# Newton-Schulz in a fast-weight kernel: its first gram from the raw momentum, and four filler stages at other places

## The chip, the cores and the metric

One core of a Trainium2 chip. The metric is the device time in microseconds (us) of one execution, the median of three runs of the kernel before.

## The reference

`x` is 2048 x 256. After a layer norm (`xn`), three things are added: `x + attn(xn) + ffn(xn)`. The attention part has a windowed softmax attention and a test-time-training layer (TTT) with four heads. TTT goes through the sequence in 16 chunks of 128 rows. In each chunk it uses its fast weights W0, W1, W2 (64 x 64 for each head), then updates them. The update is what the change touches:

```python
def _newtonschulz5(G):
    X = G
    X = X / (jnp.sqrt(jnp.sum(X * X, axis=(1, 2), keepdims=True)) + 1e-07)
    for a, b, c in NS_COEFFS:            # five of them
        A = X @ X.transpose(0, 2, 1)
        B = b * A + c * (A @ A)
        X = a * X + B @ X
    return X

def step(carry, xi):
    ...
    dw0 = dw0 + M0 * mm                  # gradient plus momentum, the same for dw1, dw2
    M0n, M1n, M2n = (dw0, dw1, dw2)
    dw0 = _newtonschulz5(dw0)
    ...
    return ((renorm(W0 + dw0, n0), ..., M0n, M1n, M2n), out)
```

The feed-forward part is a mixture of 32 experts (weights `w1`, `w2`, relu squared, routing by the top 8) and a shared expert of inner size 512, also relu squared.

## The kernel before, in words

All is float32. The sequence is taken in 16 blocks of 128 rows. Each engine has its program written out by hand, in order, and semaphores tie them together; an instruction whose semaphore is not there holds all that stands behind it on its engine. `body(i, last)` of each engine does block i and prepares block m = i + 1. The last block has no update, so there are 15 updates.

The 12 matrices of an update (4 heads x 3) are held as two groups g = 0, 1. A group is 128 partitions (two heads, one in the low 64, one in the high 64) by 3 matrices by 64 columns: `Mom[g]` (gradient plus momentum), `X[g]`, `Am[g]` (the gram), `Mp[g]`. Products of single heads are matmuls of 64x64 tiles, in one or the other quarter of the array. The PSUM of a group is `CC[g]`, two banks, `CA[g]` and `CB[g]`.

The way into Newton-Schulz, on each engine:
- TensorE: `grads` (L682) writes the six gradients of a group into CA. Then come `h_up(i, 2)`, `shared_up(i, 0)`, `sums(i, 0)`, `sums(i, 1)`, `shared_up(i, 1)` and `h_up(i, 3)`. `sums` (L693) adds the squares of a head's rows over its partitions, with a matmul by a matrix of ones in blocks.
- VectorE: `grad` (L1100) makes Mom, its squares (L1109) and their row sums (L1112). `sum_copy` (L1114) copies the summed squares from PSUM. `x_first` (L1118) adds 1e-7 to the root, takes the reciprocal and multiplies Mom by it, which is X.
- POOL (GpSimd): `ss_pow` (L335) takes the square root, as a power of 0.5.

Then come 20 stages, `st` = 0 to 19, four for each of the five steps, each done for g = 0 and g = 1. In stage 0 TensorE turns X (`ns_turn`, L697, two transposes) and ACT copies the turned one to SBUF (`xt`, L476). In stage 1 TensorE takes the gram (`ns_gram`, L703, six matmuls of 64x64) and VectorE copies it to Am (`ns_a`, L1129). In stage 2 TensorE multiplies Am by Am and VectorE makes Mp = b/c Am + the product (`ns_m`, L1134). In stage 3 TensorE multiplies Mp by X, and VectorE makes the next X (`ns_x`, L1142), with a times X from POOL (`ax`, L339).

Between the stages stands other work, the fillers. A dictionary `fill` on each engine says what follows which stage, and they have to be in the same order where they share a buffer:
- `h_up(i, u)` (L825) is the up projection of four experts into the PSUM bank HB, of which there is only one. ACT reads it with a relu into `hr` (`h_relu`, L507), and POOL squares it into `hq` (`h_sq`, L358). `y_down(i, u)` (L833) multiplies hq by the down weights into YB, and VectorE adds that to `acc` (`y_acc`, L1321).
- `shared_up` (L815) is the shared expert's up projection into M0, in two parts; ACT's `shared_relu` (L503) and POOL's `shared_sq` (L354) follow.
- `ln_norm(m)` (L998) makes `xn` of the next block on VectorE from the statistics and `rstd`, which POOL's `prep_rstd` (L287) gives. `att_scale` (L1217) scales the turned q and k with four VectorE instructions (aqT, akT). In stage 0 VectorE does these two. TensorE's `q_out` (L751), in the fillers of stage 2, waits for `e_aT` of att_scale; `prep_turn(m)` (L632) behind it begins the work on the next block.

POOL's own order in this part is k_u twice, `h_sq(i, 1)`, `ss_pow` twice, `prep_rstd(m)`, `h_sq(i, 2)`, then `ax` twice, `shared_sq`, `h_sq(i, 3)`. The change leaves it alone.

Of the kernel before, what the change touches and what calls it, by code (L numbers as in the profile page):

```python
# [27 lines left out]
ALU = mybir.AluOpType  # L28
# [4 lines left out]
P = 128  # L33
D = 256
KT = D // P
HD = 64
NH = 4
G = 2
# [18 lines left out]
NI = len(NS)  # L57
# [16 lines left out]
def build(nc, x, wall_d, rows_d, wo, fast_d, affine_d, fc1T, fc2T, e1T, e2T, upT, downT, ident_d, fixed_d, out):  # L74
# [3 lines left out]
    with ExitStack() as ctx:  # L78
# [18 lines left out]
        ident = sb("ident", [P, P])  # L97
# [178 lines left out]
        def _(pool):  # L276
# [56 lines left out]
                pool.tensor_tensor(kt[g][:, 3, :], ks[g][:, 1, :], ks[g][:, 2, :], ALU.mult).then_inc(e_ku[g], 1)  # L333

            def ss_pow(i, g):  # L335
                pool.wait_ge(e_sst[g], 3 * i + 1)
                power(r3[g][:, 2, :], r3[g][:, 1, :], half, 3).then_inc(e_pw[g], 1)

            def ax(i, g, it):  # L339
# [75 lines left out]
        def _(act):  # L415
# [12 lines left out]
            def prep_xnT(m):  # L428
                act.wait_ge(e_pt, m + 1)
                a(xnT[:, :, :].rearrange("p k t -> p (k t)"), M0[:, 0:D], ACT.Copy).then_inc(e_xnT, 1)  # L430
# [62 lines left out]
            def q_out(i):  # L493
                act.wait_ge(e_qo, i + 1)
                a(to[:, :], M1[:, 0:D], ACT.Copy)
                a(tsq[:, :], M1[:, 0:D], ACT.Square).then_inc(e_to, 1)
# [6 lines left out]
            def shared_relu(i):  # L503
                act.wait_ge(e_upm, i + 1)
                a(ur[:, :, :].rearrange("p s t -> p (s t)"), M0[:, :], ACT.Relu).then_inc(e_ur, 1)

            def h_relu(i, u):  # L507
                act.wait_ge(e_h, NU * i + u + 1)
                if u > 1 or not (isinstance(i, int) and i == 0):
                    act.wait_ge(e_hq, NU * i + u - 1)  # L510
                a(hr[u % 2][:, :, :].rearrange("p s t -> p (s t)"), HB[:, :], ACT.Relu).then_inc(e_hr, 1)
# [29 lines left out]
            def body(i, last):  # L541
                if last:
                    gate_sig(i)
                    y_first(i)
                    h_relu(i, 2)
                    shared_relu(i)
                    h_relu(i, 3)
                    q_out(i)
                    act.preload_act_table_set("natural_log_exp_and_others")
                    h_relu(i, 4)  # L550
                    probs(i)
                    h_relu(i, 5)
                    probs_T(i)
                    h_relu(i, 6)
                    h_relu(i, 7)
                    comb_T(i)
                    y_T(i)
                    return
                m = i + 1
                k_side(i, 0)  # L560
                k_side(i, 1)
                gate_sig(i)
                y_first(i)
                h_relu(i, 2)

                def to_exp():
                    act.preload_act_table_set("natural_log_exp_and_others")

                def to_sigmoid():
                    act.preload_act_table_set("sigmoid_and_others")  # L570

                shared_relu(i)
                h_relu(i, 3)
                fill = {1: [lambda: h_relu(i, 4)], 2: [lambda: q_out(i), lambda: prep_xnT(m)],
                        5: [lambda: prep_qk(m)], 6: [lambda: prep_v(m)], 7: [lambda: h_relu(i, 5), lambda: prep_small(m)],
                        8: [lambda: prep_sq8(m)], 9: [lambda: prep_vT(m), lambda: h_relu(i, 6), to_exp],
                        11: [lambda: lr_exp(m)], 12: [lambda: prep_qkT(m)],
                        13: [lambda: probs(i)], 14: [lambda: h_relu(i, 7), lambda: lr_ln(m)], 15: [lambda: probs_T(i), to_sigmoid],
                        18: [lambda: comb_T(i)], 19: [lambda: x_lat(m)]}
                for st in range(4 * NI):  # L580
                    if st % 4 == 0:
                        for g in range(G):
                            xt(i, g, st // 4)
                    for f in fill.get(st, []):
                        f()
                h_relu(m, 0)
                y_T(i)
                h_relu(m, 1)
                for g in range(G):
                    w_T(m, g)  # L590
# [24 lines left out]

        @block.tensor
        def _(pe):
            x_turn = [Expect(pe, e_x[g], f"x_turn{g}") for g in range(G)]
            xt_in = [Expect(pe, e_xt[g], f"xt_in{g}") for g in range(G)]
            am_in = [Expect(pe, e_am[g], f"am_in{g}") for g in range(G)]  # L620
            mp_in = [Expect(pe, e_mp[g], f"mp_in{g}") for g in range(G)]
# [71 lines left out]
            def sums(i, g):  # L693
                pe.wait_ge(e_s3[g], 2 * i + 2)
                mm(CB[g][:, 0:3], bdones[:, :], r3[g][:, 0, :]).then_inc(e_ssb[g], 1)

            def ns_turn(g, last_step):  # L697
                x_turn[g].wait(skip=1 if last_step else 0)
                pe.transpose(CA[g][0:HD, 0:P], X[g][:, 0, :], ident[:, :])  # L699
                pe.transpose(CA[g][:, P:2 * P], X[g][:, 1:3, :].rearrange("p w c -> p (w c)"), ident[:, :])\  # L700
                    .then_inc(e_t[g], 1)

            def ns_gram(g):  # L703

                xt_in[g].wait()
                low, high = slice(0, HD), slice(HD, P)

                def gram(out_, rows, n, c):
                    return mm(out_[c, 0:HD], XT[g][rows, n, c], XT[g][rows, n, c])

                gram(CA[g], low, 0, low)
                gram(CB[g], high, 1, high)
                gram(CA[g], low, 0, high)
                gram(CB[g], high, 1, low)
                gram(CA[g][:, 2 * P:], low, 1, low)
                gram(CA[g][:, 2 * P:], low, 1, high).then_inc(e_prod[g], 1)
# [98 lines left out]
            def shared_up(i, part):  # L815

                if part == 0:
                    pe.wait_ge(e_gh, i + 1)
                for c in range(part * SC // 2, (part + 1) * SC // 2):
                    for k in range(KT):  # L820
                        ins = mm(M0[:, c * P:(c + 1) * P], up_s[:, k, c * P:(c + 1) * P], xnT[:, k, :], k == 0, k == KT - 1)
                if part == 1:
                    ins.then_inc(e_upm, 1)
# [42 lines left out]
            def body(i, last):  # L866
# [30 lines left out]
                m = i + 1  # L897
# [5 lines left out]
                grads(i, 0)  # L903
                grads(i, 1)
                h_up(i, 2)
                shared_up(i, 0)
                sums(i, 0)
                sums(i, 1)
                shared_up(i, 1)
                h_up(i, 3)  # L910
                fill = {2: [lambda: q_out(i), lambda: prep_turn(m)], 3: [lambda: y_down(i, 2)],
                        4: [lambda: prep_qk(m)], 5: [lambda: prep_qk_more(m)], 6: [lambda: prep_v(m)],
                        7: [lambda: h_up(i, 5)], 8: [lambda: y_down(i, 3), lambda: prep_mom(m)],
# [6 lines left out]
                for st in range(4 * NI):  # L920
                    for g in range(G):
                        if st % 4 == 0:
                            ns_turn(g, st // 4 == NI - 1)
                            if st == 0 and g == 0:
                                y_down(i, 1)
                        elif st % 4 == 1:
                            ns_gram(g)
                            if st == 1 and g == 0:
                                h_up(i, 4)
                        elif st % 4 == 2:  # L930
                            ns_pair(g, CA, am_in, Am, Am)
                        else:
                            ns_pair(g, CB, mp_in, Mp, X)
                    for f in fill.get(st, []):
                        f()
# [32 lines left out]
        def _(dve):  # L968
# [149 lines left out]
            def x_first(i):  # L1118

                for g in range(G):  # L1120
                    dve.wait_ge(e_pw[g], i + 1)
                    nc.vector.tensor_scalar(r3[g][:, 2, :], r3[g][:, 2, :], 1e-7, None, ALU.add).then_inc(e_sst[g], 1)
                    dve.wait_ge(e_sst[g], 3 * i + 2)
                    nc.vector.reciprocal(r3[g][:, 1, :], r3[g][:, 2, :]).then_inc(e_sst[g], 1)
                    dve.wait_ge(e_sst[g], 3 * i + 3)
                    nc.vector.tensor_tensor(X[g][:, :, :], Mom[g][:, :, :],
                                            r3[g][:, 1, :].unsqueeze(2).to_broadcast([P, 3, HD]), ALU.mult).then_inc(e_x[g], 1)

            def ns_a(i, g, it):  # L1129
                dve.wait_ge(e_prod[g], 3 * NI * i + 3 * it + 1)  # L1130
                nc.vector.tensor_copy(Am[g][:, :, :], CC[g][:, 0:6 * P].rearrange("p (w c) -> p w c", w=3)[:, :, 0:HD])\  # L1131
                    .then_inc(e_am[g], 1)

            def ns_m(i, g, it):  # L1134

# [207 lines left out]
            def body(i, last):  # L1343
# [33 lines left out]
                        17: [lambda: att_out(i)], 18: [lambda: y_acc(i, 7)]}  # L1377
                for st in range(4 * NI):
                    for g in range(G):
                        if st % 4:  # L1380
                            (ns_a, ns_m, ns_x)[st % 4 - 1](i, g, st // 4)
                        if st > 10 and routing:
                            routing.pop(0)()
                    for f in fill.get(st, []):
                        f()
# [68 lines left out]
```

## Time and profile before

| | |
|---|---|
| median of 3 runs | 831.35 us (829.08 to 831.86) |
| the profiled execution | 830.14 us |
| its span, first to last instruction | 828.1 us |
| granted clock of TensorE, mean | 0.996 |
| TensorE busy (matmul) | 780.7 us, 94% |
| VectorE busy | 714.6 us, 86% |
| ScalarE (ACT) busy | 354.0 us, 43% |
| GpSimd (POOL) busy | 406.8 us, 49% |
| chain that ended last | PE 53%, DVE 33%, issue 6%, ACT 5%, POOL 2% |

PE is TensorE, PEld its weight loads, DVE is VectorE. The spans of matmuls are modelled and overlap, so a matmul row's duration is longer than the step from one to the next; the starts are what to go by. All matmuls have line 629, that of the helper `mm`, and all ACT instructions line 426, so that they are told apart by their tiles. A float32 matmul shows as two instructions.

### The profile page before, as it was taken

Reading aid. Unit: us, or ns where it says so; the run is one execution under the profiler, and the core shown is the slowest. Engines: PE = TensorE matmul, PEld = TensorE weight load, DVE = VectorE, ACT = ScalarE, POOL = GpSimd, SP = SyncE. Lnnn points to the kernel's source line nnn. Section 1 sums busy time; section 2 is a strip of 40 time slices with the busy share of each in tenths; the row PEclk is TensorE's granted clock in tenths of the full one; section 3 lists DMA queues with packets and bytes.
Section 4 is the critical chain, followed back from the end, with each engine's and each line's share of the span. In section 5 each row is a group of like instructions: output and inputs, shape, how many; then the busy total and the mean of one; then the engine's idle time right before and its main releaser. Section 6 shows DMA issues by size and latency. Waiting matters only on the chain.

```text
span 828.1 us, 24889 instructions
## 1 busy us (share of the span) xinstructions
PE 780.7 (94%) x9776; PEld 668.5 (81%) x9776; DVE 714.6 (86%) x2592; ACT 354.0 (43%) x868; POOL 406.8 (49%) x535
## 2 busy tenths in 40 slices
PE   3899999999999999999999999999999999999997
PEld 1888888888888888878888788887888888888886
DVE  4789898898988979889798897988979889898876
ACT  2544344443444434444344444444444444434533
POOL 1654555445454454544555445544465444655442
PEclk9899999999999999999999999999999999999999
DMA  8100000000000000000000000000000000000000
GB/s 321 54 3 14 9 2 21 3 13 9 2 21 2 14 8 2 21 2 15 8 3 20 2 15 9 3 21 2 15 8 2 21 2 15 8 2 15 2 15 7
DMA packets 9811, 15.09 MB, mean 18 GB/s; under 512 B 1120, under 2 KB 8928, under 8 KB 9440
## 3 DMA queue, kind: packets, MB, share of 16 engines
q1 hardware_dynamic: 7904, 7.80, 3.2%
q10 hardware_dynamic: 1792, 5.70, 1.8%
q8 instruction: 78, 1.28, 0.6%
q14 instruction: 37, 0.30, 0.1%
HBM read 11.41 MB, written 2.10 MB: 16 GB/s over the span
## 4 chain that ended last, share of the span: by engine, by line
PE 53%; DVE 33%; issue 6%; ACT 5%; POOL 2%; DMA 1%; SPq 0%; DVEq 0%
PE CC L629 18%; PE M L629 13%; PE HB L629 8%; DVE acc L1328 8%; PE YB L629 8%; DVE Wn L1175 4%; DVE Mp L1138 2%; DVE dhb L1094 2%; DVE X L1146 2%; PE CC L699 2%; DVE Am L1131 2%; POOL r L285 2%; DVE sm L1233 1%; DMA rows<-in_rows 1%; PE CC L700 1%
## 5 line engine op out<-in xcount | busy, mean ns | idle before, releaser
L363 POOL TENSOR_TENSOR hq<-hr 128x512 f32<-128x512 f32 x128 | 137.1, 1071 | 71.9 <-ACT hr L426 71.9
L285 POOL TENSOR_TENSOR r<-r,half 128x3 f32<-128x3 f32 (+1 forms) x78 | 77.9, 1011 | 155.1 <-DVE r L1116 67.9
L629 PE MATMUL HB<-xlT,e_s 128*128 128x128 f32 x1024 | 143.0, 283 | 0.4 <-ACT xlT L426 0.4
L629 PE MATMUL YB<-e_s,hq 128*128 128x128 f32 x1024 | 141.3, 281 | 1.8 <-DVE acc L1328 0.8
L629 PEld LDWEIGHTS HB<-xlT,e_s 128*128 128x128 f32 x1024 | 126.7, 193 | 6.8 <-ACT xlT L426 0.7
L1328 DVE SCALAR_TENSOR_TENSOR acc<-YB,cw,acc 128x128 f32<-128x128 f32 x448 | 125.4, 342 | 7.9 <-PE YB L629 7.9
L341 POOL TENSOR_TENSOR aX<-X,a_tile 128x192 f32<-128x192 f32 x150 | 92.9, 640 | 79.9 <-DVE X L1146 79.9
L426 ACT ACTIVATE hr<-HB 128x512 f32<-128x512 f32 x128 | 76.1, 594 | 128.5 <-PE HB L629 128.5
L629 PEld LDWEIGHTS YB<-e_s,hq 128*128 128x128 f32 x1024 | 124.2, 191 | 7.4 <-issue 4.1
L629 PEld LDWEIGHTS CC<-X,Mp 64*64 64x64 f32 x1800 | 58.3, 135 | 23.6 <-issue 11.3
L629 PEld LDWEIGHTS CC<-Am 64*64 64x64 f32 x1800 | 59.5, 134 | 21.8 <-DVE Am L1131 18.2
L426 ACT ACTIVATE XT<-CC 128x256 f32<-128x256 f32 x150 | 50.8, 381 | 59.7 <-PE CC L700 59.5
L629 PE MATMUL CC<-X,Mp 64*64 64x64 f32 x1800 | 68.6, 222 | 7.6 <-DVE Mp L1138 7.6
L629 PE MATMUL CC<-Am 64*64 64x64 f32 x1800 | 69.8, 223 | 1.9
L1146 DVE SCALAR_TENSOR_TENSOR X<-CC,aX 128x192 f32<-128x192 f32 x150 | 51.3, 352 | 13.4 <-PE CC L629 13.3
L629 PE MATMUL M<-wall,xnT 128*128 128x512 f32 (+1 forms) x128 | 56.9, 551 | 3.6 <-DMA rows<-in_rows 3.6
L629 PEld LDWEIGHTS CC<-XT 64*64 64x64 f32 x1800 | 43.2, 133 | 20.7 <-ACT XT L426 14.7
L1131 DVE COPY Am<-CC 128x192 f32<-128x192 f32 x150 | 48.4, 347 | 9.3 <-PE CC L629 8.3
L1138 DVE SCALAR_TENSOR_TENSOR Mp<-Am,CC 128x192 f32<-128x192 f32 x150 | 49.8, 351 | 7.2 <-PE CC L629 3.6
L629 PE MATMUL CC<-XT 64*64 64x64 f32 x1800 | 55.6, 232 | 0.0
L699 PE MATMUL CC<-ident,X 128*64 128x128 f32 x150 | 39.7, 281 | 0.0
L333 POOL TENSOR_TENSOR kt<-ks 128x128 f32<-128x128 f32 x30 | 13.7, 459 | 51.0 <-ACT ks L426 51.0
(180 smaller groups left out, 1525.3 us busy)
## 6 DMA issues: line engine op xcount, KB each, us to landing
xa<-in_x SPq DMA_DIRECT2D x16, 128.0 KB, 2.1
e_s<-in_e1T ACTq DMA_DIRECT2D x1, 2048.0 KB, 12.7
e_s<-in_e2T ACTq DMA_DIRECT2D x1, 2048.0 KB, 19.3
xr<-in_x SPq DMA_DIRECT2D x16, 128.0 KB, 2.2
out<-ot SPq DMA_DIRECT2D x16, 128.0 KB, 1.7
wall<-in_wall SPq DMA_DIRECT2D x1, 820.0 KB, 7.1
up_s<-in_upT ACTq DMA_DIRECT2D x1, 512.0 KB, 15.9
down_s<-in_downT ACTq DMA_DIRECT2D x1, 512.0 KB, 20.0
```

The costliest lines, as they stand in the source:

```text
L285: return pool.tensor_tensor(dst, src, expo[:, 0:n], ALU.pow)
L341: pool.tensor_tensor(aX[g][:, :, :].rearrange("p w c -> p (w c)"), X[g][:, :, :].rearrange("p w c -> p (w c)"), a_tile[:, it, :], ALU.mult ...
L363: pool.tensor_tensor(hq[b][:, :, :], hr[b][:, :, :], hr[b][:, :, :], ALU.mult).then_inc(e_hq, 1)
L426: return nc.scalar.activation(out_, in_, func, **kw)
L629: return pe.matmul(out_, lhsT, rhs, start=start, stop=stop)
L699: pe.transpose(CA[g][0:HD, 0:P], X[g][:, 0, :], ident[:, :])
L1094: tt(dhb[g][:, :], kt[g][:, 0, :], dhi[g], ALU.mult)
L1131: nc.vector.tensor_copy(Am[g][:, :, :], CC[g][:, 0:6 * P].rearrange("p (w c) -> p w c", w=3)[:, :, 0:HD])\
L1138: nc.vector.scalar_tensor_tensor(Mp[g][:, :, :].rearrange("p w c -> p (w c)"), Am[g][:, :, :].rearrange("p w c -> p (w c)"), b / c, CA[g][ ...
L1146: nc.vector.scalar_tensor_tensor(X[g][:, :, :].rearrange("p w c -> p (w c)"), CB[g][:, 0:3 * HD], NS[it][2], aX[g][:, :, :].rearrange("p w ...
L1175: ins = nc.vector.tensor_scalar(Wn[g][:, w, :], Wn[g][:, w, :], r3[g][:, 5, w:w + 1], nrm[g][:, w:w + 1], ALU.mult, ALU.mult)
L1328: ins = nc.vector.scalar_tensor_tensor(acc[:, e, :], y, w, acc[:, e, :], ALU.mult, ALU.add)
```

## The change

The first transposes of an update read Mom, not X. The first gram is therefore that of the raw momentum. VectorE computes the square of the inverse norm (one more small instruction for each group) and multiplies the gram by it where it copied it to Am. X is still made, behind Am, for the product with Mp and for `ax`. The gram's two matmuls into CB come last and wait for `sum_copy`, since the summed squares lie in CB. On TensorE `shared_up` 0 and 1 and the two `sums` stand behind the turns of stage 0, `y_down(i, 1)` behind all of them, and `h_up(i, 3)` between the two grams of stage 1, `h_up(i, 4)` behind the second. On ACT `shared_relu` goes into the fillers of stage 0 and `h_relu(i, 3)` into those of stage 1. On VectorE Am of the first step is now inside `x_first`.

```diff
@@ ss_pow (POOL)
-                pool.wait_ge(e_sst[g], 3 * i + 1)
+                pool.wait_ge(e_sst[g], 4 * i + 1)
@@ body (ACT)
-                shared_relu(i)
-                h_relu(i, 3)
-                fill = {1: [lambda: h_relu(i, 4)], 2: [lambda: q_out(i), lambda: prep_xnT(m)],
+                fill = {0: [lambda: shared_relu(i)], 1: [lambda: h_relu(i, 3), lambda: h_relu(i, 4)], 2: [lambda: q_out(i), lambda: prep_xnT(m)],
@@ ns_turn, ns_gram (TensorE)
-            def ns_turn(g, last_step):
-                x_turn[g].wait(skip=1 if last_step else 0)
-                pe.transpose(CA[g][0:HD, 0:P], X[g][:, 0, :], ident[:, :])
-                pe.transpose(CA[g][:, P:2 * P], X[g][:, 1:3, :].rearrange("p w c -> p (w c)"), ident[:, :])\
+            def ns_turn(i, g, it):
+                if it == 0:
+                    pe.wait_ge(e_G[g], i + 1)
+                    src = Mom[g]
+                else:
+                    pe.wait_ge(e_x[g], (NI + 1) * i + it + 1)
+                    src = X[g]
+                pe.transpose(CA[g][0:HD, 0:P], src[:, 0, :], ident[:, :])
+                pe.transpose(CA[g][:, P:2 * P], src[:, 1:3, :].rearrange("p w c -> p (w c)"), ident[:, :])\
...
+                if it == 0:
+                    gram(CA[g], low, 0, low)
+                    gram(CA[g], low, 0, high)
+                    gram(CA[g][:, 2 * P:], low, 1, low)
+                    gram(CA[g][:, 2 * P:], low, 1, high)
+                    pe.wait_ge(e_sst[g], 4 * i + 1)
+                    gram(CB[g], high, 1, high)
+                    gram(CB[g], high, 1, low).then_inc(e_prod[g], 1)
+                    return
@@ body (TensorE)
                 h_up(i, 2)
-                shared_up(i, 0)
-                sums(i, 0)
-                sums(i, 1)
-                shared_up(i, 1)
-                h_up(i, 3)
...
                         if st % 4 == 0:
-                            ns_turn(g, st // 4 == NI - 1)
-                            if st == 0 and g == 0:
+                            ns_turn(i, g, st // 4)
+                            if st == 0:
+                                shared_up(i, g)
+                                sums(i, g)
+                            if st == 0 and g == 1:
                                 y_down(i, 1)
                         elif st % 4 == 1:
-                            ns_gram(g)
+                            ns_gram(i, g, st // 4)
                             if st == 1 and g == 0:
+                                h_up(i, 3)
+                            if st == 1 and g == 1:
                                 h_up(i, 4)
@@ x_first, ns_a (VectorE)
                     dve.wait_ge(e_pw[g], i + 1)
                     nc.vector.tensor_scalar(r3[g][:, 2, :], r3[g][:, 2, :], 1e-7, None, ALU.add).then_inc(e_sst[g], 1)
-                    dve.wait_ge(e_sst[g], 3 * i + 2)
+                    dve.wait_ge(e_sst[g], 4 * i + 2)
                     nc.vector.reciprocal(r3[g][:, 1, :], r3[g][:, 2, :]).then_inc(e_sst[g], 1)
-                    dve.wait_ge(e_sst[g], 3 * i + 3)
+                    dve.wait_ge(e_sst[g], 4 * i + 3)
+                    nc.vector.tensor_tensor(r3[g][:, 0, :], r3[g][:, 1, :], r3[g][:, 1, :], ALU.mult).then_inc(e_sst[g], 1)
+                    dve.wait_ge(e_sst[g], 4 * i + 4)
+                    ns_a(i, g, 0)
                     nc.vector.tensor_tensor(X[g][:, :, :], Mom[g][:, :, :],
                                             r3[g][:, 1, :].unsqueeze(2).to_broadcast([P, 3, HD]), ALU.mult).then_inc(e_x[g], 1)
...
-                nc.vector.tensor_copy(Am[g][:, :, :], CC[g][:, 0:6 * P].rearrange("p (w c) -> p w c", w=3)[:, :, 0:HD])\
-                    .then_inc(e_am[g], 1)
+                product = CC[g][:, 0:6 * P].rearrange("p (w c) -> p w c", w=3)[:, :, 0:HD]
+                if it == 0:
+                    nc.vector.tensor_tensor(Am[g][:, :, :], product, r3[g][:, 0, :].unsqueeze(2).to_broadcast([P, 3, HD]),
+                                            ALU.mult).then_inc(e_am[g], 1)
+                else:
+                    nc.vector.tensor_copy(Am[g][:, :, :], product).then_inc(e_am[g], 1)
@@ body (VectorE)
-                        if st % 4:
+                        if st % 4 and st != 1:
                             (ns_a, ns_m, ns_x)[st % 4 - 1](i, g, st // 4)
```

## Rows read from the trace of the kernel before

**Rows 1.** Busy time by engine in a stretch (count), clock, DMA share, GB/s.
```profile
443.30:463.10 19.80, 19.76 (x261) 16.42 (x262) 16.19 (x52) 6.97 (x19) 10.66 (x14) 1.00 0.03 8
```

**Rows 2.** The chain of waits: start us, us, what.
```profile
448.07 0.89 PE HB L629 x8
...
450.75 1.09 PE HB L629 x8
```

**Rows 3.** Timeline of TensorE: start us, us, what, idle before.
```profile
445.67 1.06 PE L629 MATMUL M<-xnT,up_s 128*128 128x128 f32 x8
446.57 0.51 PE L629 MATMUL CC<-r,fixed 128*128 128x3 f32 x4
446.93 1.14 PE L629 MATMUL M<-xnT,up_s 128*128 128x128 f32 x8
447.91 1.06 PE L629 MATMUL HB<-xlT,e_s 128*128 128x128 f32 x8
448.84 0.30 PE L699 MATMUL CC<-ident,X 128*64 128x128 f32 x1
...
449.09 1.06 PE L629 MATMUL YB<-e_s,hq 128*128 128x128 f32 x8
449.98 0.27 PE L699 MATMUL CC<-ident,X 128*64 128x128 f32 x1
...
450.29 0.46 PE L629 MATMUL CC<-XT 64*64 64x64 f32 x12
450.68 1.16 PE L629 MATMUL HB<-xlT,e_s 128*128 128x128 f32 x8
451.77 0.46 PE L629 MATMUL CC<-XT 64*64 64x64 f32 x12
452.25 0.99 PE L629 MATMUL CC<-Am 64*64 64x64 f32 x24
453.17 0.71 PE L629 MATMUL M<-WT,gh 128*128 128x128 f32 x4
...
454.03 0.92 PE L629 MATMUL CC<-X,Mp 64*64 64x64 f32 x24
```

**Rows 4.** Timeline of VectorE, the same stretch.
```profile
446.89 0.39 DVE L1116 COPY r<-CC 128x3 f32<-128x3 f32 x2 [0.43 <-PE CC L629]
448.01 0.17 DVE L1122 TENSOR_SCALAR r<-r 128x3 f32<-128x3 f32 x1 [0.74 <-POOL r L285]
...
448.43 0.36 DVE L1126 TENSOR_TENSOR X<-Mom,r 128x192 f32<-128x192 f32 x1
...
449.25 0.36 DVE L1126 TENSOR_TENSOR X<-Mom,r 128x192 f32<-128x192 f32 x1
449.52 1.13 DVE L1001 TENSOR_SCALAR xn<-xa,mv,rstd 128x256 f32<-128x256 f32 x1
450.57 0.72 DVE L1224 TENSOR_SCALAR aqT<-M,affine 128x128 f32<-128x128 f32 x2
...
451.85 0.77 DVE L1131 COPY Am<-CC 128x192 f32<-128x192 f32 x2
```

**Rows 5.** Timeline of ACT, the same stretch.
```profile
449.00 0.60 ACT L426 ACTIVATE hr<-HB 128x512 f32<-128x512 f32 x1 [0.30 <-PE HB L629]
```

**Rows 6.** Timeline of POOL, the same stretch.
```profile
447.13 1.67 POOL L285 TENSOR_TENSOR r<-r,half 128x3 f32<-128x3 f32 x2 [4.53 <-DVE r L1116]
448.76 0.56 POOL L285 TENSOR_TENSOR rstd<-rstd,neghalf 128x1 f32<-128x1 f32 x1
449.29 1.21 POOL L363 TENSOR_TENSOR hq<-hr 128x512 f32<-128x512 f32 x1
450.46 1.18 POOL L341 TENSOR_TENSOR aX<-X,a_tile 128x192 f32<-128x192 f32 x2
```

**Rows 7.** Two lines over the whole span: ns min/median/max, first and last start.
```profile
L1001 DVE TENSOR_SCALAR xn<-xa,mv,rstd x16: 412/1130/1131, 5.9 to 757.6; 128x256 f32<-128x256 f32 x16
...
L1094 DVE TENSOR_TENSOR dhb<-kt,ks x30: 275/702/1124, 30.5 to 751.6; 128x128 f32<-128x128 f32 x30
```

More of the change, by code:

```diff
@@ L617, in _ @@
         def _(pe):
-            x_turn = [Expect(pe, e_x[g], f"x_turn{g}") for g in range(G)]
             xt_in = [Expect(pe, e_xt[g], f"xt_in{g}") for g in range(G)]
@@ L695, in sums, with ns_gram @@
                 mm(CB[g][:, 0:3], bdones[:, :], r3[g][:, 0, :]).then_inc(e_ssb[g], 1)
-            def ns_turn(g, last_step):
-                x_turn[g].wait(skip=1 if last_step else 0)
-                pe.transpose(CA[g][0:HD, 0:P], X[g][:, 0, :], ident[:, :])
-                pe.transpose(CA[g][:, P:2 * P], X[g][:, 1:3, :].rearrange("p w c -> p (w c)"), ident[:, :])\
+            def ns_turn(i, g, it):
[7 more added lines that the diff above has]
+                pe.transpose(CA[g][:, P:2 * P], src[:, 1:3, :].rearrange("p w c -> p (w c)"), ident[:, :])\
                     .then_inc(e_t[g], 1)
-            def ns_gram(g):
+            def ns_gram(i, g, it):
                 xt_in[g].wait()
```

## Prediction

> **What bounds the kernel now.** I read the busy time of one stretch first, then the chain of waits, then each engine's own list over the same stretch. The change touches only the join between the gradients and the first Newton-Schulz step, which happens once in each of the 15 blocks that update the weights (the last block of 16 has no update). So one such join is enough, and I take the one at 443.3 us. From the gradients on, for the next 19.8 us of a block of some 52 (830 / 16), TensorE is busy 19.76 of 19.80 us, VectorE 16.19 [rows 1]. The chain that ended last runs through TensorE there, and the same eight matmuls of an expert's up projection take 0.89 us between 128-row work and 1.09 us between two grams of 64x64 tiles [rows 2]: a change of tile size and back costs 0.20.
>
> TensorE's list [rows 3] shows why the norm chain costs nothing today. While VectorE and POOL go from the sums (446.57) to the first X (448.43), TensorE does shared_up part 1 (0.98) and h_up 3 (0.93), and y_down 1 lies between the two turns. The turn of X starts at 448.84, when h_up 3 has just ended. What the change can win is therefore small: h_up 3 takes 0.93 start to start where others take 0.89, so 0.04 of waiting for X; and gram 1 to the Am product takes 0.48 where the first gram takes 0.39 with a tile switch of 0.10 in it, so 0.19 of waiting for Am. Together 0.23 us a block. VectorE [rows 4] is nearly as tight as TensorE: it goes from X through xn and the four att_scale instructions into Am with no gap, and Am's first copy (451.85) ends at 452.2, just where TensorE takes it (452.25).
>
> **The change, part by part.** I lay the new order out on the clock of this block, from 445.67, where shared_up part 0 starts now. Start-to-start times are those of [rows 3].
>
> TensorE. Turn 0 of the raw momentum needs no norm: 0.25, to 445.92. shared_up 0: 0.90, to 446.82. sums 0: half of the two sums' 0.36, to 447.00. Turn 1: 0.25, to 447.25. shared_up 1: 0.98, to 448.23. sums 1: 0.18, to 448.41. y_down 1: 0.89, to 449.30, and 0.10 for the tile switch: gram 0 at 449.40. Its 0.39 brings h_up 3 to 449.79, which now stands between two grams and costs 1.09: gram 1 at 450.88, done at 451.27. The same work as before, except that h_up 3 and h_up 4 both sit inside the 64x64 stretch: one more switch, +0.20.
>
> Then a wait that is new. h_up 4 writes the one bank HB, which ACT must have read for h_up 3. Now hr starts 1.09 us after h_up 3 starts (447.91 to 449.00 [rows 3, 5]) and takes 0.60; with 0.10 for the switch ACT is done at 449.79 + 1.79 = 451.58. Only gram 1 stands between the two, so TensorE stands still from 451.27 to 451.58, with the first Am product, q_out and prep_turn behind it. h_up 4 then costs its 1.09: Am product at 452.67, and its 0.92 brings q_out to 453.59, against 453.17 now. So TensorE alone, with everything else in time, is 0.42 us a block later. The gram in its new order (four on the low rows, then two on the high ones) has no row. Its bounds are 0.39, the gram of now, and 0.92 / 2 = 0.46, six matmuls of this size in the Am product; I take 0.39, because the instructions are the same ones, and keep 0.14 for two grams. The wait of its last two matmuls for the copied sum of squares costs nothing: that copy lies over half a microsecond ahead for either group. On ACT shared_relu moves behind the two XT copies, and ends near 449.0, needed only by prep_turn after 453.
>
> VectorE. sums 1 has moved from directly behind sums 0 to 1.4 us later. The first copy now starts 0.32 after its sum starts (446.57 to 446.89 [rows 3, 4]), so copy 1 comes at 448.55, and x_first stands behind it even for group 0. For group 0 the small steps are 0.21 each (448.01 to 448.43 is two of them [rows 4]), now three with the square: from 448.78 to 449.40. The square has no row of its own; between nothing and the 0.21 of its neighbours I take 0.21, because the next step waits for it. Am 0 then waits for gram 0; the second Am copy of now begins 0.50 after its gram (gram 1 at 451.77; Am's pair ends at 452.62 and one takes some 0.36, as X does [rows 3, 4]), so Am 0 comes at 449.90. As a product with a broadcast column Am 0 has no row; its bounds are the 0.36 of X, the same product from SBUF, and the copy of now, which shows no more. X 0 is next, 0.30 later like each step of a run of such instructions, at 450.20.
>
> POOL decides now. It takes pow 1 0.24 after the copy starts (446.89 to 447.13), so at 448.79; two pows take 1.63 start to start (447.13 to 448.76), so one 0.82, and prep_rstd 0.53 (to 449.29), and behind it stands the square hq 2 [rows 6]: it starts at 448.79 + 0.82 + 0.53 = 450.14, a hair before X 0. That matters because of [rows 7]: xn takes 1130 ns in 15 of its 16 instances, each beside an hq, and 412 ns in the one that has none; dhb, like X a product of two operands in SBUF, takes 275 alone and 1124 beside an hq. In [rows 4, 6] xn starts at 449.52, and with its own 0.41 it can have run only from 450.24, 0.95 after hq began. So X 0 runs from 450.14 + 0.95 = 451.09, and VectorE goes on at 451.35.
>
> Group 1 then: two small steps, the square at 451.77. POOL has begun aX 0 at 451.55 (its input is just there), and that takes 0.59 (1.18 for two [rows 6]), so the square runs near 452.05. Am 1 at 452.15 (gram 1's result is there since 451.38), X 1 at 452.45, xn 0.28 later at 452.73, now clear of POOL and so 0.33 to the next start (its 0.41 less the 0.08 by which the next overlaps it now), then att_scale's four from 453.06, 0.32 apart (450.57 to 451.85 is 1.28 [rows 4]): the last starts at 454.02 and, 0.39 long, is done at 454.4. q_out needs their result, and prep_turn, Mp and the whole block stand behind it: 454.40 against 453.17, 1.2 us later. What xn saves (0.7) is in that.
>
> After q_out nothing takes it back: Mp follows att_scale on VectorE as closely as the product of X and Mp follows q_out on TensorE (0.86 [rows 3]), and TensorE has 0.04 us of idle in the stretch [rows 1]. **Sum:** 15 x 1.2 = 18 us on the profiled execution's 830.14 gives 848.1. The three runs' median, 831.35, is 1.2 above that execution, well inside the range.
>
> **The rivals.** A: X 0 gets in ahead of hq 2. The margin is 0.06 us, from steps known to 0.1. Then hq runs after it, from 450.55 to 451.50, and holds group 1's square; Am 1 at 451.60; X 1 is held by aX 0 to 452.05; att_scale ends at 454.02: +0.85 a block, 842.9. For it: X's second instance now starts 0.04 before hq and is not held (0.36), while that hq shows 1.21 [rows 4, 6]. The Trainium skill ("SBUF — State Buffer", the section on its two separate sides) says that the port pair of VectorE and GpSimd is an exclusive lock, whichever starts first keeping it for the whole instruction. By that the sum turns on this order alone; its clause on two SBUF inputs would also hold the product of X beside a pow, and there the trace disagrees: at 448.43, beside the pow, it took 0.36.
>
> C: the holds don't come about, POOL's order falling clear of VectorE. Then Am 1 follows gram 1 at 451.38 and att_scale ends near 453.6, as TensorE gets there: +0.42, 836.4.
>
> D: no change within what can be measured. About 0.3% (2.5 us) is what a measurement of this kernel can tell. It takes fillers in the block's last quarter, where VectorE is on the chain, to absorb the delay; against it, all of that hangs on the prep of the next block, which TensorE issues behind q_out.
>
> E, the other side: the turn and the gram really leave the norm chain, hr 3 is read in time, and att_scale ends before TensorE finishes the Am product. It needs att_scale to end before 453.0, so Am 1 by 450.8, when gram 1 has not even started by my layout. Price: the 0.23 of waits, 3.5 us in all, 826.7.
>
> **How the numbers follow.** My case 0.45, A 0.28, C 0.14, D 0.06, E 0.07. The likeliest gives 848. The range goes down to 838 (between A and C, since a block that mixes the cases lies there) and up to 853: 0.14 for the grams and 0.2 for a second hold of X 1 or xn by aX or the us square, 15 times, on 848. Faster by over 0.3%: 0.07, within: 0.06, slower: 0.87.
>
> **What would show it.** In the changed profile, block by block: X 0 at about 1 us beside hq (0.36 in A), or xn back at 0.41; h_up 4 starting 0.3 after gram 1, behind hr; q_out starting 1.2 us later against the gradients, with att_scale as its last releaser; the time between blocks up by 1.2. It is wrong if q_out starts no later than now, or if the delay at q_out is there and the time from block to block is not longer by as much.

## The result, and the profile after

| | before | after |
|---|---|---|
| median | 830.81 us (4 runs) | 846.63 us (4 runs, 845.78 to 847.28) |
| ratio | | 1.0192, 95% interval 1.0171 to 1.0213 |
| profiled execution, its span | 830.14, 828.1 | 846.44, 844.3 |

The changed kernel is 15.8 us slower; the forecast was 848 in a range of 838 to 853. In the traces the gradients of one block start 51.35 us after those of the block before it in the old kernel, and 52.45 us in the new one: 1.10 for each of the 15 updates.

The block shown here begins its gradients at 451.48; the one of [rows 3 to 6] begins at 443.30. All starts below that are called "after the gradients" have the block's own beginning taken off. First the timeline of VectorE, then of POOL, then of TensorE in the changed kernel (start us, us, what, count, idle before and what ended it):

```profile
456.54 0.16 DVE L1127 COPY r<-CC 128x3 f32<-128x3 f32 x1 [1.10 <-PE CC L626]
...
458.03 0.36 DVE L1147 TENSOR_TENSOR Am<-CC,r 128x192 f32<-128x192 f32 x1 [0.84 <-PE CC L626]
458.31 1.07 DVE L1140 TENSOR_TENSOR X<-Mom,r 128x192 f32<-128x192 f32 x1
459.30 0.15 DVE L1133 TENSOR_SCALAR r<-r 128x3 f32<-128x3 f32 x1
...
459.70 0.36 DVE L1137 TENSOR_TENSOR r<-r 128x3 f32<-128x3 f32 x1
460.10 0.36 DVE L1147 TENSOR_TENSOR Am<-CC,r 128x192 f32<-128x192 f32 x1
460.38 0.35 DVE L1140 TENSOR_TENSOR X<-Mom,r 128x192 f32<-128x192 f32 x1
460.64 0.41 DVE L1012 TENSOR_SCALAR xn<-xa,mv,rstd 128x256 f32<-128x256 f32 x1
460.96 0.72 DVE L1242 TENSOR_SCALAR aqT<-M,affine 128x128 f32<-128x128 f32 x2
461.60 0.72 DVE L1242 TENSOR_SCALAR akT<-M,affine 128x128 f32<-128x128 f32 x2
```

```profile
457.60 0.56 POOL L285 TENSOR_TENSOR rstd<-rstd,neghalf 128x1 f32<-128x1 f32 x1
458.12 1.04 POOL L363 TENSOR_TENSOR hq<-hr 128x512 f32<-128x512 f32 x1
459.46 0.59 POOL L341 TENSOR_TENSOR aX<-X,a_tile 128x192 f32<-128x192 f32 x1 [0.29 <-DVE X L1140]
```

```profile
457.43 0.45 PE L626 MATMUL CC<-XT 64*64 64x64 f32 x12
457.81 1.16 PE L626 MATMUL HB<-xlT,e_s 128*128 128x128 f32 x8
458.90 0.45 PE L626 MATMUL CC<-XT 64*64 64x64 f32 x12
459.66 1.16 PE L626 MATMUL HB<-xlT,e_s 128*128 128x128 f32 x8 [0.31 <-ACT hr L426]
460.75 0.92 PE L626 MATMUL CC<-Am 64*64 64x64 f32 x24
462.47 0.68 PE L626 MATMUL M<-WT,gh 128*128 128x128 f32 x4 [0.81 <-DVE akT L1242]
...
463.30 0.92 PE L626 MATMUL CC<-X,Mp 64*64 64x64 f32 x24
```

Read from the end: q_out (the matmul of `WT,gh`) starts 10.99 after the gradients; in [rows 3] it was 453.17 - 443.30 = 9.87. TensorE stood idle for 0.81 ahead of it, and the last of the four att_scale instructions released it. One more wait on TensorE is new, 0.31 for ACT's `hr`. On VectorE the first X takes 1.07 instead of 0.36 [rows 4]: it starts 0.19 after POOL's hq. The waits of TensorE over the whole span say that both new waits come in each of the 15 updates (us in total, times, longest):

```profile
PE M L626 <- DVE akT L1242: 12.2, 15, 0.8
...
PE HB L626 <- ACT hr L426: 4.6, 15, 0.3
```

Over the whole span (ns min/median/max), X lies between 348 and 1073 ns, while xn never takes over 412 (before, 1130 in 15 of 16 [rows 7]).

```profile
L1140 DVE TENSOR_TENSOR X<-Mom,r x30: 348/644/1073, 38.7 to 775.4; 128x192 f32<-128x192 f32 x30
...
L1012 DVE TENSOR_SCALAR xn<-xa,mv,rstd x16: 407/408/412, 5.9 to 775.7; 128x256 f32<-128x256 f32 x16
```

So POOL's square used to hold xn, where TensorE's fillers covered it but for at most the 0.19 by which the Am product waits in [rows 3], and now holds X, with nothing to cover it.

### The profile page after: what moved, and what is told of

Read it like the earlier page. It is cut to its first block, busy times and chain, and to the rows that moved or that the text cites. A ratio compares the mean times of both kernels' runs of the same rounds, so it can differ in the third digit from the quotient of the medians.

```text
span 844.3 us, 24949 instructions
## 1 busy us (share of the span) xinstructions
PE 780.5 (92%) x9776; PEld 667.6 (79%) x9776; DVE 716.5 (85%) x2622; ACT 354.1 (42%) x868; POOL 406.7 (48%) x535
## 4 chain that ended last, share of the span: by engine, by line
PE 46%; DVE 39%; issue 7%; ACT 5%; POOL 2%; DMA 1%; DVEq 0%; SPq 0%
PE CC L626 15%; PE M L626 13%; PE YB L626 8%; DVE acc L1346 8%; PE HB L626 5%; DVE Wn L1193 4%; DVE X L1140 2%; DVE Mp L1156 2%; DVE dhb L1105 2%; DVE X L1164 2%; DVE Am L1150 2%; PE CC L701 2%; POOL r L285 2%; DVE sm L1251 1%; PE CC L702 1%
## 5 line engine op out<-in xcount | busy, mean ns | idle before, releaser
L363 POOL TENSOR_TENSOR hq<-hr 128x512 f32<-128x512 f32 x128 | 134.5, 1051 | 71.9 <-ACT hr L426 71.9
L1150 DVE COPY Am<-CC 128x192 f32<-128x192 f32 x120 | 38.0, 348 | 8.4 <-PE CC L626 8.4
L426 ACT ACTIVATE sig<-M 128x512 f32<-128x512 f32 (+1 forms) x32 | 15.7, 490 | 54.5 <-PE M L626 54.4
```

The lines of the kernel that those rows point to most:

```text
L363: pool.tensor_tensor(hq[b][:, :, :], hr[b][:, :, :], hr[b][:, :, :], ALU.mult).then_inc(e_hq, 1)
L426: return nc.scalar.activation(out_, in_, func, **kw)
L1150: nc.vector.tensor_copy(Am[g][:, :, :], product).then_inc(e_am[g], 1)
```

## The experiments

Theory H is that of the forecast: VectorE's queue, with the hold of X 0 in it, brings att_scale late, and q_out waits for that. T puts the loss on TensorE alone, S on the second sum of squares. Ratios are to the kernel before, run on the same chip. "Block" is the time from one block's gradients to the next's in the trace.

| run | median us | ratio (95%) | block us | q_out after the gradients |
|---|---|---|---|---|
| before | 830.81 | | 51.35 | 9.87 |
| after | 846.63 | 1.0192 (1.0171 to 1.0213) | 52.45 | 10.99 |
| e1_square_ahead | 838.22 | 1.0100 (1.0083 to 1.0116) | 51.83 | 10.39 |
| e2_sum_ahead | 840.11 | 1.0117 (1.0100 to 1.0134) | 52.00 | 10.55 |
| e3_up3_ahead | 862.94 | 1.0398 (1.0347 to 1.0449) | 52.61 or 54.1 | 11.17 |
| e4_scale_between | 833.47 | 1.0043 (1.0026 to 1.0060) | 51.59 | 10.11 |
| e5_raw_alone | 869.40 | 1.0460 (1.0430 to 1.0490) | 52.81 or 54.3 | 11.36 |
| e6_scale_and_square | 834.41 | 1.0053 (1.0039 to 1.0067) | 51.59 | 10.11 |
| e7_scale_and_up3 | 829.24 | 0.9988 (0.9979 to 0.9997) | 51.19 | 9.70 |
| e8_best | 822.88 | 0.9915 (0.9901 to 0.9929) | 50.88 | 9.39 |
| e9_before_scale | 841.60 | 1.0140 (1.0123 to 1.0157) | 52.00 | 10.52 |

**e1: POOL's square ahead of the pows.**

```diff
 # POOL, body, on the changed kernel
                 h_sq(i, 1)
+                h_sq(i, 2)
                 for g in range(G):
                     ss_pow(i, g)
                 prep_rstd(m)
-                h_sq(i, 2)
```

> The changed kernel with POOL's square hq 2 ahead of the two pows instead of behind them. Theory H (a hold on VectorE: the first X waits for the hq beside it, and att_scale, which q_out waits for, stands behind it): X 0 takes 0.36 instead of 1.07, q_out starts some 10.2 to 10.3 us after the gradients instead of 10.99, 0.7 to 0.75 a block comes back, 835.5 us. Rival T (TensorE alone: the wait of h_up 4 for hr and one more change of tile size): nothing on TensorE has moved, so 846.6. Rival S (the second sum of squares comes too late): nothing has moved there either, 846.6.

The timeline of VectorE in e1, whose block begins at 445.05:

```profile
451.88 0.35 DVE L1140 TENSOR_TENSOR X<-Mom,r 128x192 f32<-128x192 f32 x1
452.14 0.16 DVE L1133 TENSOR_SCALAR r<-r 128x3 f32<-128x3 f32 x1
...
452.55 0.36 DVE L1137 TENSOR_TENSOR r<-r 128x3 f32<-128x3 f32 x1
453.07 0.36 DVE L1147 TENSOR_TENSOR Am<-CC,r 128x192 f32<-128x192 f32 x1 [0.15 <-PE CC L626]
```

X 0 starts at the same 6.83 after the gradients as in the changed kernel and takes 0.35. 0.60 of q_out's 1.12 comes back and 8.4 us of the 15.8. T and S said 846.6 and fall as accounts of the whole: TensorE's order and the sums are as they were. I had said 835.5, from 0.70 to 0.75 at q_out. Some 2 of the missing 2.7 us are that Am 1 then waits for gram 1, and xn and att_scale behind it still end 0.2 after TensorE is ready; the rest lies between the median and the profiled execution (837.4).

**e2: the second sum ahead of shared_up 1.**

```diff
 # TensorE, stage 0, on the changed kernel
-                            if st == 0:
+                            if st == 0 and g == 0:
                                 shared_up(i, g)
                                 sums(i, g)
+                            if st == 0 and g == 1:
+                                sums(i, g)
+                                shared_up(i, g)
```

> The changed kernel with the second sum of squares ahead of shared_up 1, 0.9 us earlier. H: pow 1 and so hq 2 start some 1.0 earlier (hq near 5.7 us after the gradients, over by 6.7), X 0 at 6.83 is free at 0.36; the square of group 1 may be held by aX to about 7.8, which costs nothing since gram 1 is there at 7.9; q_out near 10.3, 836 us. T: 846.6. S: 836 as well (only this run and the one before together part S from H: S wants e1 unchanged).

The timelines of VectorE and of POOL in e2 (block at 446.57):

```profile
453.40 0.63 DVE L1143 TENSOR_TENSOR X<-Mom,r 128x192 f32<-128x192 f32 x1
...
452.78 1.04 POOL L363 TENSOR_TENSOR hq<-hr 128x512 f32<-128x512 f32 x1
```

A miss in size that turned out the better test. The pow of group 1 now queues behind that of group 0, so hq starts 0.43 earlier than in the changed kernel (6.21 against 6.64 after the gradients), not 1.0, and X 0 is held for part of it: 0.63. q_out comes 0.44 earlier as well. With e1 there are three doses at one and the same start of X 0: 1.07, 0.63 and 0.35 long give q_out at 10.99, 10.55 and 10.39. The last step is smaller because from there on Am 1 waits for its gram. For S this run alone would speak (it said 836), but e1 gave back more with the sum left where it was: as far as these runs show, the late sum costs by putting hq beside X 0.

**e3: h_up 3 ahead of y_down 1.**

```diff
 # TensorE, on the changed kernel (and h_relu(i, 3) one stage earlier on ACT)
                             if st == 0 and g == 1:
+                                h_up(i, 3)
                                 y_down(i, 1)
...
-                            if st == 1 and g == 0:
-                                h_up(i, 3)
```

> The changed kernel with h_up 3 ahead of y_down 1, so that h_up 4 waits for nothing and both grams stand together (one change of tile size and back less). H: TensorE is ready for q_out 0.5 earlier (about 9.6 after the gradients) and waits for att_scale all the same; gram 0 comes 0.9 later, X 0 comes as hq ends and is not held, but aX holds the square of group 1: q_out near 11.1, 848 us (846 to 850). T: the wait of 0.44 and the switch of 0.2 are gone, 837.

TensorE's wait for hr is gone, and T's 837 became 862.9. q_out came at 11.17 (11.1 expected) and its wait at TensorE was 1.40 long. The undisturbed blocks take 52.61, 0.16 more than the changed kernel's, as H had it; 15 x 1.26 on 830.7 is 849.6. The other 13 us neither theory had. Nearly all of them come with TensorE's clock, shown here by stretch (length, then busy us of PE, PEld, DVE, ACT, POOL, granted clock, DMA share, GB/s) and by its timeline:

```profile
309.00:310.20 1.20, 0.45 (x4) 0.48 (x5) 1.20 (x5) 0.00 (x0) 1.20 (x2) 1.00 0.36 109
310.40:313.60 3.20, 3.20 (x33) 2.75 (x32) 1.98 (x7) 0.94 (x3) 0.61 (x2) 0.50 0.00 0
313.80:317.00 3.20, 3.20 (x35) 1.62 (x34) 2.23 (x9) 0.66 (x2) 2.68 (x4) 1.00 0.00 0
```

```profile
309.75 0.68 PE L626 MATMUL M<-WT,gh 128*128 128x128 f32 x4 [1.40 <-DVE akT L1241]
...
310.79 1.55 PE L626 MATMUL CC<-X,Mp 64*64 64x64 f32 x24
312.27 1.83 PE L626 MATMUL YB<-e_s,hq 128*128 128x128 f32 x8
```

TensorE stood idle for 1.40, worked again from 309.75, and from 310.4 to 313.6 had half its clock (1.2 GHz, not 2.4). The product of X and Mp took 1.55 instead of 0.92. Of the 15 waits of this length 8 were followed by such a fall, which makes the block 54.13 to 54.26 instead of 52.61. 8 x 1.52 = 12.2, which on 849.6 gives 861.8 against the 862.9 measured.

**e4: att_scale between the copies of the two sums.**

```diff
 # VectorE, on the changed kernel (and att_scale out of the fillers of stage 0)
                 sum_copy(i, 0)
+                att_scale(i)
                 sum_copy(i, 1)
                 x_first(i)
```

> The changed kernel with the four att_scale instructions moved on VectorE from behind x_first to the idle time between the copies of the two sums. H: copy 1 comes 0.2 later (5.3), which moves hq 2 behind the start of X 0, and q_out has nothing to wait for but TensorE itself: 10.2 after the gradients, 0.3 later than in the kernel before, 835.5 us. T (all of the loss is TensorE's): 846.6. S: the second sum is later still, so 846.6 or more.

The timelines of VectorE, POOL and TensorE in e4 (block at 443.36):

```profile
450.18 1.17 DVE L1140 TENSOR_TENSOR X<-Mom,r 128x192 f32<-128x192 f32 x1
...
452.08 0.36 DVE L1147 TENSOR_TENSOR Am<-CC,r 128x192 f32<-128x192 f32 x1
...
450.10 1.04 POOL L363 TENSOR_TENSOR hq<-hr 128x512 f32<-128x512 f32 x1
...
452.62 0.92 PE L626 MATMUL CC<-Am 64*64 64x64 f32 x24
453.47 0.71 PE L626 MATMUL M<-WT,gh 128*128 128x128 f32 x4
```

q_out at 10.11 (10.2 expected) and 833.5 us, 2 less than expected. The hold, which I had said would go, is 1.17 here. It costs nothing: of what q_out needs only Am 1 stands behind it, and that is done at 9.08, ahead of the second half of the Am product (9.66). What is left against the kernel before, 0.24 a block and 0.43% in time, is TensorE's own share of the loss. By the terms of the forecast it is the wait for hr (0.31) and the switch of tile size (0.20), less some 0.27 that the new order saves; this run does not part these.

**e5: the raw gram alone.** All four fillers on TensorE (`shared_up` with `sums`, `y_down(i, 1)`, `h_up(i, 3)`, `h_up(i, 4)`) and the two relus on ACT are back where the kernel before has them, VectorE is that of the change.

```diff
 # TensorE, on the changed kernel; ACT's shared_relu and h_relu(i, 3) likewise ahead of the stages
                 h_up(i, 2)
+                shared_up(i, 0)
+                sums(i, 0)
+                sums(i, 1)
+                shared_up(i, 1)
+                h_up(i, 3)
...
-                            if st == 0:
-                                shared_up(i, g)
-                                sums(i, g)
-                            if st == 0 and g == 1:
+                            if st == 0 and g == 0:
                                 y_down(i, 1)
...
                             if st == 1 and g == 0:
-                                h_up(i, 3)
-                            if st == 1 and g == 1:
                                 h_up(i, 4)
```

> The raw gram alone: all fillers on TensorE and ACT where the kernel before has them. H: gram 0 comes some 1.0 us later than in the changed kernel, and xn and att_scale stand behind both Am products on VectorE; no square holds X 0 (hq 2 is over by 7.0), yet q_out comes near 11.4 after the gradients, 1.5 to 1.6 later than before: 854 us, and up to 12 more where TensorE's clock falls in the idle stretch ahead of q_out, as it did in e3 after one of 1.5 us. T: no extra switch and no wait for hr, so TensorE has nothing against it: 831 or a little less.

869.4 us, the slowest. No X is held here (all 30 at 347 to 359 ns), yet q_out is at 11.36: with the gram 1.0 later, the queue of Am, X, xn and att_scale ends later by itself. The undisturbed blocks take 52.81, and 11 of 15 have the fall of the clock: 15 x 1.46 + 11 x 1.52 = 38.6, measured 39.0. (The wait ahead of q_out is 1.39 to 1.40 in e3 and here, not the 1.5 that the expectation names.) The moves of the fillers therefore take back a large part of what the raw gram costs (1.46 a block without them, 1.10 with them, both at full clock); the hold is one item in the queue and not the root of it.

**e6: e4 and e1 together.** The two diffs are those above.

> e4 (att_scale between the copies) with e1 (the square ahead of the pows) on top. H: in e4 the hold of X 0 was still there (1.17) but nothing on the way to q_out stood behind it; freeing it brings nothing, q_out at 10.1, 833.5 us as in e4. A rival by which the hold costs its 0.7 wherever it stands would give 823.

The same block, 51.59, with every X at 347 to 350 ns and not 1.17 us for the first one. The hold costs what stands behind it and is late by it, and here nothing is.

**e7: e4 and e3 together.** The two diffs are those above.

> e4 with e3 (h_up 3 ahead of y_down 1) on top. With att_scale out of the way TensorE sets q_out, and now its wait for hr (0.44) and one switch (0.2) are gone: q_out near 9.65 after the gradients (9.87 in the kernel before), no idle stretch of TensorE over 0.3 us and so no fall of the clock; 827 to 829 us. If e3's loss was h_up 3's place itself and not the queue on VectorE, it shows here too: 848 or more.

829.2, ratio 0.9988, the change of e3 that cost 16 us on the changed kernel now gains 4 (against e4). The place of h_up 3 was never the trouble. In its trace the second half of the Am product waits for Am 1 (9.21 after the gradients, the first half starts at 8.55).

**e8: a version that beats both.** e7 with e1's order on POOL, and on VectorE:

```diff
 # VectorE, x_first
             for g in range(G):
                 dve.wait_ge(e_pw[g], i + 1)
                 ...                              # + 1e-7, reciprocal, square, as in the change
-                dve.wait_ge(e_sst[g], 4 * i + 4)
-                ns_a(i, g, 0)
-                nc.vector.tensor_tensor(X[g][:, :, :], Mom[g][:, :, :], ...)
+            for g in range(G):
+                dve.wait_ge(e_sst[g], 4 * i + 4)
+                ns_a(i, g, 0)
+            for g in range(G):
+                nc.vector.tensor_tensor(X[g][:, :, :], Mom[g][:, :, :], ...)
```

> e7 with the square ahead of the pows and, on VectorE, the small steps of both groups first, then both Am products, then both X. H: Am 1 is there before TensorE wants it, q_out at 9.5, 825 us (824 to 828), faster than both kernels. If the second group's Am was in time in e7 already, the same as e7.

822.9 us, 0.85% faster than the kernel before and 2.8% faster than the changed one. The timeline of TensorE in its block at 488.15:

```profile
494.99 0.68 PE L626 MATMUL CC<-XT 64*64 64x64 f32 x24
495.61 1.16 PE L626 MATMUL HB<-xlT,e_s 128*128 128x128 f32 x8
496.69 0.92 PE L626 MATMUL CC<-Am 64*64 64x64 f32 x24
497.54 0.71 PE L626 MATMUL M<-WT,gh 128*128 128x128 f32 x4
498.09 0.38 PE L633 MATMUL M<-ident,xn 128*128 128x128 f32 x2
498.40 0.92 PE L626 MATMUL CC<-X,Mp 64*64 64x64 f32 x24
```

No wait stands in it. The two grams run as one stretch, and q_out is at 9.39, 0.48 ahead of the kernel before; that is the 0.47 by which the block is shorter. POOL still holds xn for 0.27 there (682 ns), which prep_turn does not notice. Against e7 this run changes two orders at once, POOL's and VectorE's, and no run shows how much of the 0.31 between them belongs to which.

**e9: att_scale ahead of x_first, without the raw gram.** In the kernel before the copies of the two sums follow each other, so there is no idle time between them as in e4; the nearest place is VectorE's wait for the pow.

```diff
 # VectorE, on the kernel before (and att_scale out of the fillers of stage 0)
                 sum_copy(i, 1)
+                att_scale(i)
                 x_first(i)
```

> The kernel before (gram of the normalised X) with att_scale ahead of x_first, in VectorE's wait for the pow. If the gain of e8 were that of att_scale's place alone, this gains as well, 825 or so. By H it doesn't: the wait there is only 0.7 long and att_scale 1.3, so X 0 comes 0.6 later and TensorE's turn, which in this kernel needs X, with it (at 6.1 after the gradients instead of 5.54); 0.2 of that comes back at the Am product; 836 us. The raw gram is what makes room for it.

841.6 us, so that place alone is no gain; it loses more than the 836 that I had said. X 0 comes at 5.58 after the gradients and the turn at 6.00 (5.54 before), and then X 1 falls into hq (0.95 long) and its turn comes 0.6 late too, at 7.30. Am 1 follows at 9.61, and that sets q_out.

## Why the prediction was right

**The bound.** That TensorE alone sets this stretch, and that the norm chain is covered, held: the raw gram as it was put in wins nothing by itself (e5). The "0.23 a block" of waits as the most to be won was too small, though only for other edits: e8 wins 0.47 to 0.48. By the starts on TensorE, 0.25 of that lies in the two grams, which stand together (0.62 against 0.39 and 0.48), 0.28 in the turns, the sums and the shared_ups, and 0.07 in the Am product; h_up 3 and y_down 1 take 0.13 more. h_up 3 takes 0.97 there with no turn behind it, so the 0.04 that the forecast called a wait for X is not shown to be one.

**TensorE's own part**, forecast as 0.42: the Am product starts 9.27 after the gradients, against 8.95, so 0.32. The wait of h_up 4 was 0.31 beyond the switch, as laid out; the last 0.1 is that the shared_ups, the sums and the turns take 0.22 less in their new order than the shares taken from [rows 3], of which y_down 1 with its switch and gram 1 give 0.13 back. The gram in its new order takes 0.38 (457.43 to 457.81), the lower bound. At q_out TensorE's part is smaller still, 0.24: e4, where q_out waits for nothing, has it at 10.11, as the Am product takes 0.84 from start to start and not 0.92.

**The hold.** Forecast: hq at 6.84 after the gradients, X 0 at 6.90, so held, by a margin of 0.06. Measured: 6.64 and 6.83. The order was right, in 15 of 15 updates, and the margin three times what I gave. With steps known to 0.1 a forecast margin of 0.06 did not decide the order, so that it came out this way was in part luck, as the chance of 0.45 says. Rival A, with X 0 first, did not happen once, and C (836.4) would have needed what e1 made by hand (838.2). X 0 ended at 7.90 after the gradients against 8.15 forecast. The square of group 1 ran 0.36 long beside aX, as forecast.

**The sum.** The last att_scale instruction starts 10.44 after the gradients, 0.28 earlier than forecast (454.02 - 443.30 = 10.72), mostly since hq had started 0.20 earlier, behind a sum that came 0.19 earlier; q_out is only 0.11 earlier (10.99 against 11.10), as TensorE takes 0.15 to follow, which I had left out. 1.10 a block was measured for 1.2. The term that was mis-sized is the end of VectorE's queue, by 0.1 a block at q_out, 1.5 us in all; the 0.28 and the 0.15 partly cancel, which was luck.

**Nothing takes it back** later in the block (rival D): 1.12 at q_out, 1.09 at the product of X and Mp, 1.10 from block to block. In every run a block with TensorE at its full clock is longer or shorter by what q_out is later or earlier, within 0.05 (e1: 0.52 and 0.48; e8: 0.48 and 0.47).

**The shares of the 1.12**, by the runs: 0.60 is the hold (e1), 0.28 the rest of VectorE's queue (from e1 to e6), 0.24 TensorE's order. The last two are differences of runs and depend on the order in which the edits are undone. Rival E's gain exists, but not at its place: it needed att_scale out of the queue (e4), h_up 3 ahead of y_down 1 (e7) and Am 1 ahead of X 0, with POOL's square ahead of the pows (e8).

## What to carry to other kernels

When a wait is taken out of one engine's path, look at what stood behind it on the other engines: a queue in order that gets a new wait in its middle passes it on to all that follows, and here the victim was att_scale, which has nothing to do with the norm. Work without inputs from the chain belongs into the chain's idle time (VectorE waited 1.10 for the second sum here), which only exists once the chain is off the path of the busiest engine. A hold of one engine by another costs what stands behind it: the same hold cost 0.6 us a block in the changed kernel and nothing in e4.

## What the runs showed of the hardware that I had not expected

- **A wait of 1.4 us can halve TensorE's clock.** In e3 and e5 TensorE waits 1.39 to 1.40 us ahead of q_out; 8 and 11 of 15 such waits were followed by a stretch at 1.2 GHz, at 1.52 us each. With a wait of 0.81 in the same place (the changed kernel) none was. A loss of this kind comes on top of the wait and is larger than it. The length of one wait does not settle it: the one of 1.46 ahead of the first gradients, in the traces of before and after, had no fall behind it, and two of 0.86 and 0.95 close together in the last block had one in the traces of e1, e3, e5 and e7 and none in the seven others. What decides is open.
- **POOL's hold ends before POOL's instruction does, by the profile.** X 0 starts at 458.31 and takes 1.07, of which 0.35 are its own, so it ran from 459.03, 0.91 after hq began, while hq is shown with 1.04. In e2 and e4 the same sum gives 0.90. By the earliest rows I had taken 0.95.
- **A product of 128x3 elements is held too**, beside aX, which the forecast had assumed without a row for it: 0.36 instead of 0.16 (452.55 in e1), though X beside a pow, which is also POOL's, is not [rows 4, 6].
